# A six-stage transformer block on one core: the dense stages' last batches written out, and the attention's factor table made by GpSimd in the stage before

## What is computed

```python
x = x + 0.5 * L0_ffn(ln(x))    # 64 experts, top 3
x = x + L0_attn(ln(x))         # windowed attention with learned bonds
x = x + 0.5 * L0_ffn(ln(x))
x = x + 0.5 * L1_ffn(ln(x))    # 8 experts, top 2, and a shared one: "dense stage"
x = x + L1_attn(ln(x))         # causal attention, 16 heads of 16
x = x + 0.5 * L1_ffn(ln(x))    # dense stage again; its result is the output
```

```python
def L1_ffn(x):
    scores = sigmoid(x @ gate_W) * route_scale              # 8 scores a token
    v, i = top_k(scores, 2);  gate = onehot(i) weighted by v / sum(v)
    y = gelu(x @ W1[e] + b1[e]) @ W2[e] + b2[e]             # all 8 experts on all tokens
    return sum over e of gate[e] * y[e]  +  gelu(x @ Ws1 + bs1) @ Ws2 + bs2

def L1_attn(x):
    dist = clip(|key - query|, 0, 16)
    scores = (q @ k.T) * rel_emb[dist]                      # a factor per distance
    return softmax(causal(scores) / sqrt(16)) @ v @ Wo + bo
```

## Time and profile before

| | us |
|---|---|
| median of three runs | 3115.01 (3107.58, 3115.89, 3115.01) |
| profiled execution | 3107.8 |
| its span, first to last instruction | 3106.1 |
| first dense stage, VectorE's first to last work | 1921.6 to 2227.9 |
| causal attention | 2229.4 to 2806.9 |
| last dense stage | 2807.8 to 3102.1, then the last store |
| TensorE busy | 2824.6 (91%) |
| VectorE, ScalarE, GpSimd busy | 1674.6, 1556.4, 1317.7 |

### The profile page before, as it was taken

How to read it: one execution, slowest core, us unless ns; L and a number is a source line. 1 busy time by engine, 2 the same in 40 slices (tenths; PEclk the granted TensorE clock), 3 DMA queues, 4 the chain that set the end, 5 groups by cost and what they waited for, 6 DMA issues and landing times. The chain is left out here.

```text
span 3106.1 us, 54232 instructions
## 1 busy us (share of the span) xinstructions
PE 2824.6 (91%) x19419; PEld 2032.8 (65%) x19419; DVE 1674.6 (54%) x4656; ACT 1556.4 (50%) x2621; POOL 1317.7 (42%) x1315
## 2 busy tenths in 40 slices
PE   6899999877898988588999998999879999998999
PEld 5799999732444443368999996666546566655676
DVE  5411111288888888363111112677776666666666
ACT  1133333369899898311333332333257777783333
POOL 5444444379888888163444442000043443320000
PEclk9899999889999999768999998999989999999999
DMA  8299999705566555862999997000052333301000
GB/s 288 73 327 328 325 329 325 224 16 37 59 60 65 56 62 62 97 201 86 326 325 328 328 326 228 5 1 1 25 133 72 78 98 94 91 1 39 14 14 20
DMA packets 360543, 432.23 MB, mean 139 GB/s; under 512 B 86721, under 2 KB 315238, under 8 KB 357222
## 3 DMA queue, kind: packets, MB, share of 16 engines
q1 hardware_dynamic: 334902, 394.66, 48.0%
q0 software_dynamic: 24576, 33.57, 5.1%
q10 hardware_dynamic: 816, 0.79, 0.1%
HBM read 356.08 MB, written 72.88 MB: 138 GB/s over the span
## 5 line engine op out<-in xcount | busy, mean ns | idle before, releaser
L1806 ACT ACTIVATE f_h_t<-f_h_ps,f_b_t 128x128 f32<-128x128 f32 x1024 | 319.6, 363 | 596.3 <-PE f_h_ps L1764 596.0
L2186 POOL TENSOR_TENSOR a_dmg_buf<-a_c 128x2048 f32<-128x2048 f32 x128 | 519.9, 4096 | 77.8 <-PE a_dmg_ps L2250 48.4
L1764 PEld LDWEIGHTS f_h_ps<-f_rows_t,f_w 128*128 128x128 f32 x4096 | 482.8, 194 | 9.9 <-issue 3.5
L1764 PE MATMUL f_h_ps<-f_rows_t,f_w 128*128 128x128 f32 x4096 | 483.9, 277 | 2.3 <-DVE f_rows_t L1820 1.2
L1778 PE MATMUL f_y_ps<-f_w,f_h_t 128*128 128x256 f32 x2048 | 483.4, 379 | 0.0
L1724 POOL DMA_INDIRECT acc_rows<-f_y,f_give x128 | 205.0, 1602 | 487.6 <-DMA acc_rows<-f_y,f_give 441.1
L1778 PEld LDWEIGHTS f_y_ps<-f_w,f_h_t 128*128 128x128 f32 x2048 | 369.8, 190 | 39.9
L1820 DVE COPY f_rows_t<-f_t_ps 128x256 f32<-128x256 f32 x128 | 54.3, 424 | 597.9 <-PE f_t_ps L1752 597.9
L2562 DVE SCALAR_TENSOR_TENSOR a_bond_buf<-a_a,a_small_rep,a_q_ps 128x512 f32<-128x512 f32 x512 | 346.6, 739 | 8.0 <-PE a_q_ps L2380 4.2
L999 ACT ACTIVATE a_prob<-a_prob,a_neg_top 128x384 f32<-128x384 f32 (+3 forms) x512 | 276.5, 570 | 46.7 <-POOL a_neg_top L816 46.5
L536 DVE SCALAR_TENSOR_TENSOR x_resid<-f_y_ps,f_gate,x_resid 128x256 f32 x512 | 216.7, 478 | 122.5 <-PE f_y_ps L384 111.9
(11 more groups left out here) (358 smaller groups left out, 4135.4 us busy)
## 6 DMA issues: line engine op xcount, KB each, us to landing
f_w<-in_L_ffn_w_dram SPq DMA_DIRECT2D x256, 1024.0 KB
a_skewed<-skew SPq DMA_DIRECT2D x32, 512.0 KB, 6.8
a_k_s<-parts SPq DMA_DIRECT2D x16, 768.0 KB, 7.8
acc_rows<-x_resid SPq DMA_DIRECT2D x17, 512.0 KB, 7.8
xn_rows<-f_xn SPq DMA_DIRECT2D x16, 512.0 KB, 3.6
a_vals<-val_rows SPq DMA_DIRECT2D x64, 128.0 KB, 3.9
skew<-a_bond SPq DMA_DIRECT2D x128, 64.0 KB
x_resid<-acc_rows SPq DMA_DIRECT2D x30, 256.0 KB, 7.0
```

Of the source, the lines that this page charges most:

```text
L1764: last = nc.tensor.matmul(h_ps[n // HB][:, (n % HB) * P:(n % HB + 1) * P], w1_sb[s][:, c, n * P:(n + 1) * P], rows_t[e % 2][:, c, :], star ...
L1806: nc.scalar.activation(h_t[k][:, n, :], h_ps[n // HB][:, (n % HB) * P:(n % HB + 1) * P], ACT.Gelu, bias=b1_t[:, n, e:e + 1]).then_inc(gelu ...
L2186: nc.gpsimd.tensor_tensor(dmg_buf[n % RING][:, :, :], places(c_sb[h], first_place(dg)), c_sb[h][:, PAD:].unsqueeze(1).broadcast_to([P, DG, ...
```

## The change

It has three parts. In `ffn1_phase` the loops of TensorE, ScalarE and VectorE take three iterations, and the last two batches are written out behind them; the eighth (`more=False`) prepares no ninth. VectorE's `add` of the biases of the eighth batch gives `half_done` after each half, with a drain, and in the last stage SP stores that batch in two halves. And the attention's `factor` moves out of `attn1_phase`: the dense stage ahead of it gets `table`, SP loads `rel_emb` there behind the biases, and GpSimd makes the table behind its constants. The attention keeps only the mask and identity casts, whose drain gives `mask_ready`.

```diff
@@ ffn1_phase, sync
+            if table is not None:
+                sp.dma_start(rel_sb[:, :], rel_emb.partition_broadcast(P)).then_inc(rel_loaded, 16)
             if out_dram is not None:
-                for i in range(B):
+                for i in range(B - 1):
                     sp.wait_ge(batch_done, i + 1)
                     sp.dma_start(out_dram[i].rearrange("(j p) d -> p j d", p=P), core.x_batch(i)).then_inc(stored, 16)
-                sp.wait_ge(stored, 16 * B)
+                for half in range(2):
+                    sp.wait_ge(half_done, half + 1)
+                    sp.dma_start(out_dram[B - 1, half * S // 2:(half + 1) * S // 2, :].rearrange("(j p) d -> p j d", p=P),
+                                 core.x_batch(B - 1)[:, 2 * half:2 * half + 2, :]).then_inc(stored, 16)
+                sp.wait_ge(stored, 16 * (B + 1))
@@ ffn1_phase, gpsimd, behind const_ready
+            if table is not None:
+                near = factor[:, S - NEAR:]
+                nc.gpsimd.iota(dist[:, :], pattern=[[-1, NEAR]], base=CLIP, channel_multiplier=1,
+                               allow_small_or_imprecise_dtypes=True)
+                nc.gpsimd.memset(factor[:, :], 0.0).then_inc(table_step, 1)
+                pool.wait_ge(table_step, 1)
+                nc.gpsimd.tensor_scalar(dist[:, :], dist[:, :], float(CLIP), -1.0, ALU.min, ALU.max).then_inc(table_step, 1)
+                pool.wait_ge(table_step, 2)
+                nc.gpsimd.tensor_scalar(near, dist[:, :], -1.0, None, ALU.is_equal).then_inc(table_step, 1)
+                pool.wait_ge(rel_loaded, 16)
+                for n in range(CLIP + 1):
+                    pool.wait_ge(table_step, 3 + 2 * n)
+                    nc.gpsimd.tensor_scalar(hit[:, :], dist[:, :], float(n), rel_sb[:, n:n + 1], ALU.is_equal,
+                                            ALU.mult).then_inc(table_step, 1)
+                    pool.wait_ge(table_step, 4 + 2 * n)
+                    nc.gpsimd.tensor_tensor(near, near, hit[:, :], ALU.add).then_inc(table_step, 1)
+                nc.gpsimd.tensor_scalar(factor[:, 0:S - NEAR], factor[:, 0:S - NEAR], rel_sb[:, CLIP:CLIP + 1], None,
+                                        ALU.add).then_inc(table_step, 1)
+                pool.wait_ge(table_step, 4 + 2 * (CLIP + 1))
+                nc.gpsimd.tensor_scalar(factor[:, :], factor[:, :], scale, None, ALU.mult)
@@ ffn1_phase, tensor (scalar and vector alike)
-            with pe.Fori(0, B // 2) as pair:
...
+            def batch(i, k, more=True):
+                for n in range(NE):
+                    if n + 1 < NE:
+                        up(i, k, n + 1)
+                    down(i, k, n)
+                    if n == 3:
+                        turn_gates(i)
+                    if more and n in (4, 5):
+                        norm.pe_transpose(i + 1, chunks=(n - 4,))
+                    if more and n == 6:
+                        logits(i + 1, 1 - k)
+                biases(i, k)
+                if more:
+                    up(i + 1, 1 - k, 0)
+            with pe.Fori(0, B // 2 - 1) as pair:
+                for k in range(2):
+                    batch(pair * 2 + k, k)
+            batch(B - 2, 0)
+            batch(B - 1, 1, more=False)
@@ ffn1_phase, vector, add()
                     last.then_inc(y_free, 1)
+                    if n == NE and isinstance(i, int) and i == B - 1:
+                        nc.vector.drain().then_inc(half_done, 1)
@@ attn1_phase, tensor
-            pe.wait_ge(tables_ready, 1)
+            pe.wait_ge(mask_ready, 1)
@@ attn1_phase, vector (the load of rel_emb on SP and the iota on GpSimd go too)
-            def tables_begin():
+            def copy_mask():
                 nc.vector.tensor_copy(mask_b[:, :], mask_f)
                 nc.vector.tensor_copy(ident_b[:, :], core.ident[:, :])
...
+                nc.vector.drain().then_inc(mask_ready, 1)
...
-            tables_begin()
-            dve.wait_ge(rel_loaded, 16)
+            copy_mask()
             take("xn", 0, 0)
             take("xn", 1, 0)
             inverse_std(TPB, LATER, 2)
-            tables_add(0, 5)
             take("q", 0, 0)
-            tables_add(5, 8)
             take("k", 0, 0)
             take("q", 1, 0)
             take("k", 1, 0)
-            tables_add(8, 12)
             take("v", 0, 0)
-            tables_add(12, CLIP + 1)
             take("v", 1, 0)
-            tables_end()
```

More of the change, by code:

```diff
@@ L19 @@
 EPS = 1e-5
+HEAD_DIM = D // 16
 def due(count):
@@ L304, in ffn1_phase @@
         stored = sem("stored")
+        half_done = sem("half_done")
+        if table is not None:
+            factor, rel_emb, scale = table
+            CLIP = rel_emb.shape[0] - 1
+            NEAR = P + CLIP
+            rel_sb = sb("rel", [P, CLIP + 1])
+            dist = sb("dist", [P, NEAR])
+            hit = sb("hit", [P, NEAR])
+            rel_loaded = sem("rel_loaded")
+            table_step = sem("table_step")
         block = ctx.enter_context(nc.Block())
@@ L441, in _, with batch @@
             sigmoid(0)
-            with act.Fori(0, B // 2) as pair:
-                for k in range(2):
-                    i = pair * 2 + k
-                    for n in range(1, NE):
-                        gelu(i, k, n)
-                        if n == 2:
-                            norm.act_std(i + 1)
-                        if n == 7:
-                            sigmoid(i + 1)
-                    gelu(i + 1, 1 - k, 0)
+            def batch(i, k, more=True):
+                for n in range(1, NE):
+                    gelu(i, k, n)
+                    if more and n == 2:
+                        norm.act_std(i + 1)
+                    if more and n == 7:
+                        sigmoid(i + 1)
+                if more:
+                    gelu(i + 1, 1 - k, 0)
+            with act.Fori(0, B // 2 - 1) as pair:
+                for k in range(2):
+                    batch(pair * 2 + k, k)
+            batch(B - 2, 0)
+            batch(B - 1, 1, more=False)
         @block.vector
@@ L552, in _, with batch, attn1_phase @@
                 core.wait_x(dve, i)
-            with dve.Fori(0, B // 2) as pair:
-                for k in range(2):
-                    i = pair * 2 + k
-                    for n in range(NE + 1):
-                        add(i, k, n)
-                        if n == 0:
-                            norm.dve_stats(i + 1)
-                        if n == 0:
-                            split_first(k)
-                        if n == 1:
-                            split_second()
-                        if n == 2:
-                            norm.dve_normalise(i + 1)
-                        if n == 3:
-                            copy_gates(i)
-                        if n in (4, 5):
-                            norm.dve_copy_t(i + 1, 1 - k, chunks=(n - 4,))
-                        if n == 7:
-                            gates(i + 1, 1 - k)
-                    nc.vector.drain().then_inc(batch_done, 1)
+            def batch(i, k, more=True):
+                for n in range(NE + 1):
+                    add(i, k, n)
+                    if more and n == 0:
+                        norm.dve_stats(i + 1)
+                    if n == 0:
+                        split_first(k)
+                    if n == 1:
+                        split_second()
+                    if more and n == 2:
+                        norm.dve_normalise(i + 1)
+                    if n == 3:
+                        copy_gates(i)
+                    if more and n in (4, 5):
+                        norm.dve_copy_t(i + 1, 1 - k, chunks=(n - 4,))
+                    if more and n == 7:
+                        gates(i + 1, 1 - k)
+                nc.vector.drain().then_inc(batch_done, 1)
+            with dve.Fori(0, B // 2 - 1) as pair:
+                for k in range(2):
+                    batch(pair * 2 + k, k)
+            batch(B - 2, 0)
+            batch(B - 1, 1, more=False)
 MASKED = -1e30
-def attn1_phase(core, name, parts_dram, wq, wk, wv, wo, bo, rel_emb):
+def attn1_phase(core, name, parts_dram, factor, wq, wk, wv, wo, bo):
     nc = core.nc
@@ L678, in attn1_phase @@
         bo_sb = sb("bo", [P, D])
-        rel_sb = sb("rel", [P, CLIP + 1])
-        factor = sb("factor", [P, S])
         mask_b = sb("mask_b", [P, P], BF16)
@@ L698, in attn1_phase @@
         wqk_sb = [prob[:, k, :].rearrange("p (c n) -> p c n", c=DC) for k in range(2)]
-        dist = prob[:, 2, 0:NEAR]
-        hit = [prob[:, 3 + k, 0:NEAR] for k in range(2)]
         mask_f = prob[:, 5, 0:P]
@@ L2856, in macaron @@
             if ph == "a1":
-                attn1_phase(core, f"a1_{n}", parts, *[t["L1_attn_" + s] for s in
-                            ("Wq", "Wk", "Wv", "Wo", "bo", "rel_emb")])
+                attn1_phase(core, f"a1_{n}", parts, factor, *[t["L1_attn_" + s] for s in
+                            ("Wq", "Wk", "Wv", "Wo", "bo")])
         core.free_semaphores()
```

49 lines of the change are left out of this document (8 added, 41 removed).

## The result

The changed kernel took 3078.82 us (median of 5 runs, 3076.2 to 3081.58) against 3107.58 us (5 runs, 3100.35 to 3115.89) of the kernel before beside it: ratio 0.9912, 95% interval 0.9891 to 0.9933. Its profiled execution took 3076.2 us, with a span of 3074.3.

The account below looks back on a forecast made before the run. It took TensorE, busy nearly throughout both dense stages, as their bound. Terms 5.2 + 0.6 + 5.2 + 2.1 + 4.9 - 0.7 gave 17.3 us; against the median 3115.0 that is 3097.7, stated as 3097.5, range 3087 to 3106.

Parts of the forecast that it names:

- Ninth batch, last stage, with the store: End of last stage: dropping ninth-batch work on TensorE and VectorE gains 5.2 us, storing the last batch in halves 0.6.
- Ninth batch, first dense stage: End of first dense stage: VectorE ends earlier, the attention still starts 1.54 us later; gain 5.2 us.
- One iteration less: First dense stage's loop: two jumps back to code fetched again, not three; gain 2.1 us (0 to 2.3).
- the ends of batches 5 and 6: First dense stage: two rows, at 2080.05 and 2116.83, read as batch ends 36.78 us apart.
- Attention's prologue: Without table steps on VectorE, TensorE's wait before the second batch's transposes shrinks from 13.8 to about 9 us; gain 4.9.
- The table's price: First dense stage: GpSimd's table steps delay VectorE's steps in the first batch; loss 0.7 us (0 to 5).
- The prediction's beginning of the table: First dense stage: GpSimd begins the table once rel has landed, at about 1946 us.
- two levels 8 us apart: Whole kernel before: runs of 3107.58, 3115.89 and 3115.01 us read as two levels, the profile on the lower.
- the unlucky place in the last stage: Rival: the last stage's loop lands where jumps refetch code, two at 2.1 us each; 3101.9 us, chance 0.12.
- too long by little: Argument against the last-stage refetch rival: the unlucky place is too long by little, and the new one must hit that again.

Follow-up runs that it names:

- ninth_kept: The changed kernel with its last batch again making everything for the ninth; first dense stage 308.2 us, last stage 301.2 us.
- tail_only: The kernel before with only the written-out batches and half stores, the table staying in the attention's prologue; 3088.61 us, ratio 0.9956.
- table_only: The kernel before with only the factor table moved to GpSimd in the first dense stage; 3096.01 us, ratio 0.9978.
- padded kernel before: The kernel before with 20 drains more on VectorE in the first dense stage, in its wait for the bias loads; 3097.57 us, ratio 0.9984.
- Hit_last: The changed kernel with 74 drains more on VectorE in the last stage only; 3092.22 us, ratio 0.9959.
- pad_first: The changed kernel with 20 drains more on VectorE in the first dense stage; 3075.94 and 3074.94 us in two measurements, ratios 0.9923 and 0.9903.
- before_third: The kernel before, unchanged, profiled a third time; its layer-0 attention took 716.4 us.

## Why the prediction was right in its steps and wrong in its number

Term by term, predicted and measured, like for like:

- **Ninth batch, last stage, with the store: 5.2 + 0.6 = 5.8.** Measured 5.7 to 6.1 in the stage; ninth_kept says 5.2, the store 0.5. Right.
- **Ninth batch, first dense stage: 5.2.** 5.2 by ninth_kept. What the step missed is the barrier: it held the 1.54 us between VectorE's last addition and the attention's first step for fixed. It is 1.11 now, 1.09 in tail_only and 1.58 in table_only. That looks like a price of ending a stage with the loop's last pass, but the padded kernel before ends so too:

```profile
2217.63 1.41 DVE L1038 BATCH_NORM_STATS2 a_stats<-x_resid 128x6 f32<-128x256 f32 x4 [1.16 <-PEq L52]
```

So the 0.4 us go with the loop's place as well: they show only where a loop in the unlucky place ends the stage.
- **One iteration less: 2.1.** Three jumps cost 6.4 us in the kernel before by the distances of the batches' ends (36.65, 36.78 and 36.61 for 34.54), 2.1 each, and its padded form is 6.3 us shorter in the stage. Right, and the cause, the fetch, is now shown by moving it. The two rows that the prediction calls the ends of batches 5 and 6 are those of the fourth and fifth; the distance is the same.
- **Attention's prologue: 4.9.** The gap shrank by 4.87 (13.84 to 8.97); TensorE's first score product behind it starts 4.9 us earlier by the stage's clock. The whole stage averages 577.1 us in the six profiles that have the table in its prologue and 571.5 in the twelve that don't: 5.6, with single profiles 3 us apart. Right, a little short.
- **The table's price: 0.7.** VectorE's extra busy time is 0.75 us, of which 1.3 were allowed and half set on the path; what reaches the stage's length is within its scatter of 0.5 us. Right in size and too small to place further. The prediction's beginning of the table holds too: 1946 us, 26.5 us into the stage, measured 26.3.

The sum by stages is 5.8 + 7.6 + 5.6 = 19.0 us against the predicted 17.3 (7.6 being dense 1, 309.7 less 302.1).

The step that failed is the last, the base from which the sum was taken and the range around it: "Against the median 3115.0 the sum gives 3097.7", with "two levels 8 us apart" and the profiled execution "on the lower". The kernel before has a median of 3103.1 us over 56 runs, 11.9 us below 3115.0, and that is 12 of the 18.7 us between forecast and result. 1.7 us more are the terms above, and the rest is what stays open. There are no two levels but a continuum of 22 us (3093.5 to 3115.9). The profile, taken for the lower level, lies at 3107.8 us itself 4.7 above the median, and its layer-0 attention, 724.2 us, is the longest of all; that stage alone differs by 12 us in four profiles of this kernel. That TensorE spends 125 us of it at the lower clock and waits 29 us for one load could be read before; what was not drawn from it is that such a stage has no fixed length.

Two things stay open here. The two highest of the 56 runs, 3115.89 and 3115.01, are both among the three that were shown; the other 53 reach 3112.3 at most. Three such draws by chance would be rare, so that something may have held the kernel before higher in just that measurement; the changed kernel beside it was not (3079.0 in the mean there, 3080.2 over all its runs). No run here decides that. And the base does not explain the range alone: 3103.1 less the 21 us that the prediction held possible at most is 3082.1, and the result lies 3.3 us below it.

**Open**: 4 to 5 us. The whole runs differ by 23.4 plus or minus 2.6 us, the stages by 19. The four untouched stretches together average 1914.2 us in the four profiles of the kernel before and 1910.6 in the three of the changed one, with single profiles from 1898.5 to 1921.9 us over all builds. These 3.6 us would close most of the rest, but a small systematic gain of the build there is neither shown nor excluded.

Of the rivals, the unlucky place in the last stage did not come about: the loop begins 48 into a block. Hit_last shows that it was a real one, at 4.9 us for two jumps where 4.2 were set. The edge was closer than the argument "too long by little" knew, since tail_only stood at 109.

## What to carry to other kernels

When a stage shortens, ask what follows its last useful instruction on each engine: the pipeline's preparation of a batch that doesn't exist cost 2.6 us on TensorE and as much again on VectorE, at the end of each of the two stages. A loop body that only just fits what an engine keeps of its code is a matter of place: a late start behind every jump, named by the profile as a wait for an engine that had long been done, with packets on the instruction queue beside it, is taken away by twenty cheap instructions ahead of the loop, or by writing the loop out. And before a forecast is set against a median of three, look how much of the kernel runs at the lower clock: here it was a sixth of a long stage, and the median of three lay 12 us above that of 56.

## What the runs showed of the hardware

- VectorE goes back within a loop of 267 instructions without a fetch (no packet in pad_first), or with one of three or four packets of 8 KB and some 4.5 us late, depending on the place of the loop's start; twenty drains more or less decide it.
- The same 5487 matmul records of one stage were busy from 587.5 to 599.2 us in different executions, with the granted clock; the stage took 707 to 724 us. In before_third the busy time was 599.2 us in a stage of 716.4: busy time alone does not tell the length either.
- Two-input and scalar steps of GpSimd beside VectorE cost VectorE 0.75 us for 36 steps that take 25 us, and three times as much for three times the steps.
- Drains of VectorE that follow one another cost 0.04 to 0.05 us each (20 in 0.96 us, 37 in 1.44 and 1.63). The 20 in a wait for a load delayed nothing that shows; 37 outside a wait delayed the first addition by 1.2 to 1.5 us.
- The step over the barrier behind the first dense stage took 1.55 to 1.58 us where a loop in the unlucky place ends the stage, and 1.04 to 1.22 in all other profiles.
